# A gated cross-attention and top-2 expert kernel: first masks in six pieces, q transposed later, normalising ahead of scatters, tails cleared after 14 batches

## The reference, cut to what matters

```python
# x: 16 batches x 100 queries x 128; ctx: 16 x 1444 keys x 128; 8 experts, F = 512
xn  = layernorm(x)
att = xn @ w_input.T + (xn * dot_scale) @ ctx.T - 1e30 * mask[:, None, :]
x   = x + tanh(g_xattn) * softmax(att) @ ctx
xn2 = layernorm(x)
p   = softmax(xn2 @ W_router.T); gates, experts = top_k(p, 2); gates /= gates.sum()
y   = sum over e of weight_e * ((silu(xn2 @ W_gate[e].T) * (xn2 @ W_up[e].T)) @ W_down[e].T)
x   = x + tanh(g_ffn) * y
```

## Time and profile before

| what | value |
|---|---|
| time, median of 3 runs | 282.87 us (278.66, 282.87 and 322.13) |
| profiled execution: time | 280.85 us |
| profiled execution: span, first to last instruction | 278.8 us |
| PE busy | 242.4 us, 87% of the span |
| DVE, ACT, POOL busy | 144.4, 137.0, 112.2 us (52%, 49%, 40%) |
| chain that ended last | PE 70%, DMA 8%, issue 6%, DVE 5%, ACT 4%, POOL 4% |
| mean granted TensorE clock | 0.946 of full speed |
| one step of the steady attention | about 8.2 us (scores of batches 11 and 12 start at 103.52 and 111.69 us in the chain) |

### The profile page before, as it was taken

The page is one execution under the profiler, slowest core; times in us unless marked ns, Lnnn a source line. Parts: engine busy times, 40 slices in busy tenths (PEclk is TensorE's granted clock), DMA queues, the critical chain, the costliest instruction groups (busy, mean ns, idle before and its releaser), DMA issues.

```text
span 278.8 us, 5798 instructions
## 1 busy us (share of the span) xinstructions
PE 242.4 (87%) x1614; PEld 198.3 (71%) x1615; DVE 144.4 (52%) x467; ACT 137.0 (49%) x302; POOL 112.2 (40%) x197
## 2 busy tenths in 40 slices
PE   6799999999999999999978599699999999998100
PEld 6557777788777788777778387588888888887100
DVE  3434666767777767787746338223433343432024
ACT  3445455676555686655545234345545555545000
POOL 3250432157644476636374535433424223233200
PEclk9989999999999999999979979989999999999855
DMA  5875787778787888888632003221211111000164
GB/s 134 223 199 149 186 218 195 187 210 228 200 244 210 214 191 207 206 218 225 246 76 49 15 2 91 63 70 58 58 39 45 54 38 38 28 19 31 34 218 119
DMA packets 17645, 36.49 MB, mean 131 GB/s; under 512 B 3692, under 2 KB 9460, under 8 KB 17620
## 3 DMA queue, kind: packets, MB, share of 16 engines
q1 hardware_dynamic: 13580, 31.36, 43.4%
q0 software_dynamic: 2560, 3.77, 4.5%
q10 hardware_dynamic: 1480, 1.05, 1.2%
HBM read 30.89 MB, written 5.27 MB: 130 GB/s over the span
## 4 chain that ended last, share of the span: by engine, by line
PE 70%; DMA 8%; issue 6%; DVE 5%; ACT 4%; POOL 4%; SPq 0%; POOLq 0%; DVEq 0%; ACTq 0%
PE psum L1067 14%; PE psum L1046 13%; PE psum L1170 9%; PE psum L1022 7%; PE psum L1148 6%; PE psum L1150 5%; PE psum L1149 5%; PE psum L1159 4%; DMA ctx_sb<-results 3%; PE psum L1057 2%; DMA slots<-pair_rows,slot_i 2%; ACT probsT L616 2%; POOL slots L527 2%; DMA results<-y_sb,dest 2%; ACT qT L611 1%
## 5 line engine op out<-in xcount | busy, mean ns | idle before, releaser
L583 POOL DMA_INDIRECT results<-y_sb,dest x32 | 30.7, 959 | 57.1 <-DVE dest L948 25.6
L1067 PE MATMUL psum<-ctx_sb,probsT 120*100 120x128 f32 (+1 forms) x384 | 49.2, 280 | 0.0
L959 DVE SCALAR_TENSOR_TENSOR scores<-probs,row_in,psum 128x512 f32<-128x512 f32 x32 | 23.9, 747 | 42.6 <-ACT probs L691 41.3
L1067 PEld LDWEIGHTS psum<-ctx_sb,probsT 120*100 120x100 f32 (+1 forms) x384 | 44.9, 172 | 0.3 <-issue 0.2
L1046 PE MATMUL psum<-ctxT,qT 128*100 128x512 f32 (+1 forms) x96 | 43.2, 587 | 0.0
L527 POOL DMA_INDIRECT slots<-pair_rows,slot_i x32 | 33.5, 1046 | 22.6 <-DVE slot_i L846 8.4
L691 ACT ACTIVATE probs<-psum 128x512 f32<-128x512 f32 x32 | 19.1, 598 | 39.0 <-PE psum L1150 39.0
L1170 PE MATMUL psum<-w_down,hidT 128*128 x256 | 34.3, 277 | 0.8 <-ACT y_sb L706 0.6
L782 DVE CUSTOM_DVE_ANT_0 scores<-psum,maskb 100x1444 f32<-100x1444 f32 x16 | 26.6, 1660 | 13.3 <-PE psum L1046 13.3
L1170 PEld LDWEIGHTS psum<-w_down,hidT 128*128 128x128 f32 x256 | 31.5, 194 | 1.2 <-issue 1.2
L1148 PE MATMUL psum<-w_hi,rowT_hi 128*128 x64 | 29.1, 454 | 2.4 <-issue 1.0
(11 more groups left out here) (138 smaller groups left out, 372.2 us busy)
## 6 DMA issues: line engine op xcount, KB each, us to landing
ctx_sb<-in_ctx SPq DMA_DIRECT2D x16, 720.0 KB
maskb<-mask_scaled SPq DMA_DIRECT2D x14, 564.1 KB
w_raw<-in_w_experts SPq DMA_DIRECT2D x16, 256.0 KB, 6.0
row_in<-slots SPq DMA_DIRECT2D x32, 65.0 KB, 1.9
...
```

What stands on the lines that cost most here:

```text
L583: nc.gpsimd.indirect_dma_start(results, bass.IndirectOffsetOnAxis(ap=dest[:, s:s + 1], axis=0), y_sb[:, s, :], None).then_inc(y_stored[s], 16)
L1067: last = nc.tensor.matmul(attn_ps[0:Q, 0:D], probsT[0:rows[c], c, :], ctx_sb[0:rows[c], b % RING, c, :], start=(c == 0), stop=(c == CHUNKS ...
```

## The change

- First masks: the mask is padded to 1536 columns and read as 512-column pieces. ScalarE scales 38 rows x 512 in one instruction (rows 0 to 31 and, again, the six pieces at rows 32 to 37); VectorE turns rows 32 to 37 into the low halves. `select` picks high and low row together, so `add_mask` has three matmuls in place of six, and batch 0's runs ahead of `transpose_q(0)`. Scaling and storing the whole mask comes after ScalarE's evictions of context 0; context 3 is loaded behind the first `load_mask`. The tanh moves behind the first exponential, and the four warming matmuls of step 0 go.
- `transpose_q(b + 1)` moves from ahead of the transposed probabilities to behind the first group of `attend(b - 1)`, and ScalarE's copy of it to just ahead of the exponential.
- The router work of batch 13 (`transpose_xn2(13)`, `route(13)`, `top_two(13)`, `choose(6)`) leaves step 15 for the stretch behind it, as does batch 14's and 15's by about one place each; attention of batch 15 is no longer split around `transpose_rows(0, 1)`.
- GpSimd: scatter 10 moves to the head of loop step 15; normalise 14 goes ahead of scatter 12, normalise 15 ahead of scatter 13.
- Tails: 328 rows behind the counts after 14 batches, all eight by SP right after its first eight row loads, and scatter 14 (not `load_rows`) waits for them.
- `transpose_rows(8)` and its two halves move behind `transpose_hidden(6)`. The late tables are spread over tiles 3 to 6. The last four result scatters don't wait for earlier ones.

```diff
-SP_TAILS = 6
+TAIL_ROWS = 328
+TAIL_PART = 82
+    PIECES = 3
+    PIECE = mask.shape[1] // PIECES
+    LOW = 32
+    assert PIECE == 512 and K <= PIECES * PIECE and MASKED * PIECES <= LOW
+    SPREAD = TAIL_ROWS // TAIL_PART
+    assert TAIL_ROWS >= (TOKENS - PARTS[-2][1] * Q) + P - 1 and PARTS[-2][1] * Q + TAIL_ROWS <= REGION
...
-select = sb("select", [B, MASKED, Q], F32R)
-mask_hi = w_hi[0:B, 0:K]
-mask_lo = w_lo[0:B, 0:K]
+first_rows = LOW + MASKED * PIECES
+select = sb("select", [first_rows, MASKED * PIECES, Q], F32R)
+first_raw = w_lo[0:first_rows, 0:PIECE].bitcast(F32)
+first_split = w_hi[0:first_rows, 0:PIECE]
...
+    pieces = mask.rearrange("b (t n) -> (b t) n", n=PIECE)
     load_x(0)
-    sp.dma_start(mask_rows, mask).then_inc(mask_raw, 16)
+    sp.dma_start(first_raw[0:LOW, :], pieces[0:LOW, :]).then_inc(first_loaded_mask, 16)
+    sp.dma_start(first_raw[LOW:first_rows, :], pieces[0:MASKED * PIECES, :]).then_inc(first_loaded_mask, 16)
     load_ctx(0)
     load_x(1)
+    sp.dma_start(mask_rows, mask[:, 0:K]).then_inc(mask_raw, 16)
     load_ctx(1)
     load_x(2)
     load_ctx(2)
-    load_ctx(RING - 1)
     sp.wait_ge(mask_stored, 16)
     load_mask(MASKED)
+    load_ctx(RING - 1)
     load_x(3)
...
         n = i * YRING + k
         if k == EARLY:
             sp.wait_ge(late_ready, 1)
-            sp.wait_ge(tails_stored, 16 * E)
             sp.wait_ge(empty_stored, 16)
...
     def clear_tail(e):
-        at = sp.value_load(tail_row[0:1, e:e + 1], min_val=0, max_val=DUMMY)
-        sp.dma_start(slots[bass.ds(at, P), :], empty[:, :]).then_inc(tails_stored, 16)
+        at = sp.value_load(tail_row[0:1, e:e + 1], min_val=0, max_val=DUMMY - TAIL_ROWS)
+        sp.dma_start(slots[bass.ds(at, TAIL_ROWS), :].rearrange("(p r) d -> p r d", r=SPREAD),
+                     empty[0:TAIL_PART, :, :]).then_inc(tails_stored, 16)
...
-            for e in range(SP_TAILS):
+            for e in range(E):
                 clear_tail(e)
...
     for b in range(B):
+        if b == B - 1:
+            pair_landed(0)
+            scatter(b - 5)
         if b >= 2:
             root2(b - 2)
             normalise2(b - 2)
         if 5 <= b < B - 1:
             scatter(b - 5)
-        if b == B - 2:
-            pair_landed(0)
-        if B - 2 <= b:
-            scatter(b - 4)
         if b == 2 or b == 6 or b == 10:
             root1(b + 2, b + 6)
         if b + 2 < B:
             normalise1(b + 2)
-    pair_landed(1)
-    scatter(12)
+    scatter(11)
     root2(B - 2)
     normalise2(B - 2)
     pair_landed(1)
-    scatter(13)
+    scatter(12)
     root2(B - 1)
     normalise2(B - 1)
+    pair_landed(1)
+    scatter(13)
     last_gates()
+    pool.wait_ge(tails_stored, 16 * E)
     pair_landed(1)
     scatter(14)
...
-        if k % 2 == 0:
+        if k % 2 == 0 and k < LOOP_END:
             wait(pool, y_stored[(k - 1) % YRING], i * 16 + 16 * ((k + YRING - 1) // YRING) if k else 0)
...
     def step(b):
-        if 0 <= b - 1 < B:
-            if b + 1 < B:
-
-                act.wait_ge(probsT_raw, (b - 1) * GROUPS + 1)
-                copy_qT(b + 1)
+        if b >= 1:
             for g in range(GROUPS):
                 copy_probsT(b - 1, g)
-        elif b == 0:
-            copy_qT(1)
         if b + 1 < B:
             evict_ctxT(b + 1, 0)
             evict_ctxT(b + 1, 1)
-        if 0 <= b - 2 < B - 2:
+        if 0 <= b - 2 < B - 3:
             copy_xn2T(b - 2)
+        if b + 1 < B:
+            copy_qT(b + 1)
         if b < B:
             act.wait_ge(negmax_done, b + 1)
             nc.scalar.activation(probs[0:Q, :], scores[0:Q, :], ACT.Exp, bias=negmax[:, b % 2:b % 2 + 1],
                                  accum_out=rowsum[:, b % RING:b % RING + 1]).then_inc(probs_done, 1)
+            if b == 0:
+                act.wait_ge(small_loaded, 48)
+                nc.scalar.activation(tanh_g[:, :], gates_in[:, :], ACT.Tanh).then_inc(tanh_done, 1)
             if 4 <= b and b % 2 == 0:
                 exp_gap((b - 4) // 2)
...
     act.wait_ge(scale_loaded, 32)
     nc.scalar.activation(warm[:, :], wi_col[:, :], ACT.Exp)
+    act.wait_ge(first_loaded_mask, 32)
+    nc.scalar.activation(first_split, first_raw, ACT.Copy, scale=NEG).then_inc(mask_hi_done, 1)
+    copy_qT(0)
+    evict_ctxT(0, 0)
+    evict_ctxT(0, 1)
     act.wait_ge(mask_raw, 16)
     nc.scalar.activation(mask_rows, mask_rows, ACT.Copy, scale=NEG).then_inc(mask_scaled_done, 1)
     act.wait_ge(mask_scaled_done, 1)
     act.dma_start(mask_scaled, mask_rows).then_inc(mask_stored, 16)
-    copy_qT(0)
-    nc.scalar.activation(mask_hi, mask_rows, ACT.Copy).then_inc(mask_hi_done, 1)
-    evict_ctxT(0, 0)
-    evict_ctxT(0, 1)
-    act.wait_ge(small_loaded, 48)
-    nc.scalar.activation(tanh_g[:, :], gates_in[:, :], ACT.Tanh).then_inc(tanh_done, 1)
     for b in range(B):
         step(b)
...
     def tile_step(i, k):
         n = i * YRING + k
-        if 0 < k and k + 1 < T:
+        if 0 < k and k + 1 < T and k != EARLY - 1:
             rowT_high(i, k + 1)
+        if k == 2:
+            copy_xn2T(B - 1)
         if k < T:
             act.wait_ge(gate_up_raw, n + 1)
             wait(act, hidden_done, n - 1)
             nc.scalar.activation(silu[k % 2], gate_ps[k % 2], ACT.Silu).then_inc(silu_done, 1)
         if k == 0:
-            rowT_high(i, 1)
             copy_xn2T(B - 2)
         if 0 <= k - 1 < T:
             act.wait_ge(hidT_raw, n)
             wait(act, y_raw, n - 2)
             nc.scalar.activation(hidT[:, (k - 1) % 2, :], hidT_ps, ACT.Copy).then_inc(hidT_done, 1)
-        if k == 1:
-            copy_xn2T(B - 1)
+        if k == EARLY - 1:
+            rowT_high(i, k + 1)
         if k - 2 >= 0:
             s = (k - 2) % YRING
             act.wait_ge(y_raw, n - 1)
             wait(act, y_stored[s], i * 16 + 16 * ((k - 2) // YRING))
             nc.scalar.activation(y_sb[:, s, :], y_ps, ACT.Copy).then_inc(y_done, 1)

-    def between(n):
-        e = SP_TAILS + n - 4
-        if 0 <= n - 4 and e < E:
-            if e == SP_TAILS:
-                act.wait_ge(tails_ready, 1)
-            clear_tail(e)
-
-    exp_gap(LAST - 1)
     rowT_high(0, 0, first_rowT_ps)
-    nc.scalar.activation(warm[:, :], wi_col[:, :], ACT.Silu)
+    copy_xn2T(B - 3)
     for g in range(GROUPS):
         copy_probsT(B - 1, g)
-    over_tiles(act, tile_step, between)
+    exp_gap(LAST - 1)
+    nc.scalar.activation(warm[:, :], wi_col[:, :], ACT.Silu)
+    rowT_high(0, 1)
...
         b0, b1 = PARTS[p]
         at = ranks_of(p)
         dve.wait_ge(rank_raw, p + 1)
+        if p == LAST - 1:
+            nc.vector.tensor_copy(tail_row[:, :], at[:, N, :]).then_inc(tails_ready, 1)
         if p == LAST:
-            nc.vector.tensor_copy(tail_row[:, :], at[:, N, :]).then_inc(tails_ready, 1)
...
-        if b >= 2:
+        if 2 <= b < B - 1:
             top_two(b - 2)
-        if 3 <= b and b % 2 == 1:
+        if 3 <= b < B - 1 and b % 2 == 1:
             choose((b - 3) // 2)
         if b == 12:
+            tile_counts(False)
             tile_runs(False)
         if b == 14:
-            tile_tables(False)
+            tile_experts(False)
+            tile_rows(False)
         if 4 <= b and b % 2 == 0:
             gate_pair((b - 4) // 2)
         for c in split[1:]:
...
-    nc.vector.tensor_copy(select[:, :, :], identity[0:B, 0:MASKED].unsqueeze(2).to_broadcast([B, MASKED, Q])).then_inc(select_done, 1)
+    nc.vector.tensor_tensor(select[:, :, :], identity[0:first_rows, 0:MASKED * PIECES].unsqueeze(2).to_broadcast([first_rows, MASKED * PIECES, Q]),
+                            identity[0:first_rows, LOW:first_rows].unsqueeze(2).to_broadcast([first_rows, MASKED * PIECES, Q]),
+                            ALU.add).then_inc(select_done, 1)
...
-    nc.vector.tensor_tensor(mask_lo, mask_rows, mask_hi.bitcast(F32), ALU.subtract).then_inc(mask_lo_done, 1)
+    nc.vector.scalar_tensor_tensor(out=first_split[LOW:first_rows, :], in0=first_raw[LOW:first_rows, :], scalar=NEG,
+                                   in1=first_split[LOW:first_rows, :].bitcast(F32), op0=ALU.mult,
+                                   op1=ALU.subtract).then_inc(mask_lo_done, 1)
...
     def between(n):
         if n == 3:
+            tile_counts(True)
+        if n == 4:
             tile_runs(True)
-        if n == 4:
-            tile_tables(True)
+        if n == 5:
+            tile_experts(True)
+        if n == 6:
+            tile_rows(True)

...
     residual(B - 2)
+    statistics2(B - 2)
+    attention_gain(B - 1)
     rowT_low(0, 0, first_rowT_ps)
-    statistics2(B - 2)
+    top_two(B - 3)
+    choose(LAST - 1)
+    place(LAST - 1)
     gate_pair(LAST - 1)
-    place(LAST - 1)
-    attention_gain(B - 1)
+    rowT_low(0, 1)
     over_tiles(dve, tile_step, between)
...
     def transpose_q(b):
         pe.wait_ge(xn_done, b + 1)
+        wait(pe, ctxT_act, 2 * b + 1 if b else 0)
         nc.tensor.transpose(ring_ps[0][:, GROUP * Q:GROUP * Q + Q], xn[:, b % 2, :],
...
```

(61 more changed lines are left out.)

38 lines of the change are left out of this document (20 added, 18 removed).

## The result

The changed kernel takes 292.88 us (median; 290.63 to 293.63) beside 281.19 for the kernel before on the same chip: ratio 1.048, 95% interval 1.037 to 1.059. It is slower, where 262.0 us were forecast. The profiled execution has a span of 288.7 us where before's had 278.8.

A forecast was written before the change was run, and what follows sets the result against it. TensorE work was taken to bound the steady attention, GpSimd's in-order queue the late steps, with 13.3 us lost between 139 and 185 us. Gains 4.9 + 1.0 + 11.8 + 1.1 = 18.8 us: 280.85 to 262.0 us, range 257 to 271.

The forecast's parts named there:

- Tail clears: End of the attention: eight tails take 8 us to issue, landing near 158.5, before scatter 14 wants them.
- Rival D: Tail clears through SP hold scatter 14; slower than before beyond 3.7 us each, 286.5 us at 4.4 each; chance 0.04.
- First masks: Start of the kernel: earlier mask halves and three mask matmuls bring scores 0 and 1 forward; gain 4.9 us.
- rival B: Start: the clock stays low, scores 0 keep 4.21 us and another such stretch costs 1.6; 265.2 us, chance 0.12.
- The third term: Start: from the end of scores 0 to scores 1 takes about 2.9 us instead of 4.35; gain 1.4 us.
- Rival C: Early attention: the DMAs starve batch 2 or 3, losing about 2 to 3 us; 265 us, chance 0.08.
- q: Attention steps: q transposed later lets ScalarE start 0.3 us earlier per step; gain 1.0 us, between 0 and 2.0.
- End of the attention: From exponential 15 to `gate_up(8)`: reordered late work gains 12.5 us, 11.8 after a charge for slower GpSimd steps.
- less 0.4 because attention 15 now starts behind the first expert tile and `ranks(6)`: End of the attention: deduction from xn2(15)'s gain of 6.3 us, leaving minus 5.9, at about 152.5.
- rival A: Late chain: in-order queues keep half, slips and a clock fall leave 6 of 12.5 us; 268.5 us, chance 0.2.
- The charge of 0.7 us for slower GpSimd steps: End of the attention: normalise 14 and 15 slow beside VectorE, taking 0.7 us off the gain, bounds 0 and 1.5.
- End: Last result scatters: without waits scatter 31 starts near 259.35 instead of 260.42; gain 1.1 us.

The follow-up runs named there:

- 84-part run: The changed kernel with each tail as 336 rows cut in 84 parts of 4 rows instead of 328 in 82 of 4: 275.75 us, ratio 0.986.
- the one with the old start: The kernel with 112 parts, its whole new start undone to that of the kernel before, later q kept: 272.01 us, ratio 0.972.
- 112 parts: The changed kernel with each tail as 336 rows cut in 112 parts of 3 rows instead of 328 in 82 of 4: 273.36 us, ratio 0.978.
- the run with earlier tables: The kernel with 112 parts, late tile tables made behind tiles 3 to 5 instead of 3 to 6: 269.95 us, ratio 0.966.
- the runs with a mended start: Two on the kernel with 112 parts: context 0 loaded ahead of mask pieces, 271.43 us (0.971); more warming matmuls in TensorE's early pauses, 272.80 us (0.979).

## Why the prediction was wrong, point by point

- **Tail clears: the step that failed, and it decides.** "At 1 us each they are free", and "eight take 8". I took the price of a tail from the six of before, each of 128 parts, and scaled it by nothing. 82 rows on two engines cost 4 us each (147.7 to 179.9 us for eight). Rival D had the wait right: `tails_stored`, and 3.7 us a tail as the point from which the kernel is slower. At the 4.0 us measured its own sum gives some 283 us; the profiled execution took 290.63, and the rest is the other misses below. What D lacked was the reason, and so its chance was 0.04. "DMAs that are 0.08 busy" was no argument against it: idle engines do not help a transfer that is not given to them. The divisors of 82 would have said so without a run.
- **First masks, -4.9 forecast, -0.6 measured.** The parts that concern the masks hold: both halves by 6.1 us, three matmuls at 6.20. "The evictions then wait for the transposes alone" is true, but the transposes wait for context 0, whose load I had not priced. With context 0 first the forecast start of scores 0 appears (10.61). "I take it that the clock holds" failed in this execution: rival B. Its price was right at the start of the attention (3.2 us; 3.0 between two executions of the same start, scores 1 at 20.52 and 17.55), and nothing of it is left at the end, since the loads set the pace. The third term, 1.4, held (2.96 us against 2.9).
- **Rival C,** the starved batches, was right as a mechanism but named batch 2 or 3. It strikes at batch 4 or 8 where the start is quick, and the idle DMAs from 17 to 20 us are the ones that I had let context 3 wait through. But a quick start is not its only condition: a wait of 1.8 us for context 12 stands also in the 84-part run and in the one with the old start, whose scores 1 started at 20.11 and 22.02, and the latter loads context 3 early. What decides it there is open.
- **q, -1.0 forecast.** Mechanism right, size off: 2.5 us where nothing disturbs it, above my bound of 2.0, for the gap of 0.15 us is there in each step and a further 0.09 is saved at the router's matmul in every second one. In the kernel after, other waits leave 0.5 of it.
- **End of the attention, -11.8 forecast, -7.8 with 112 parts.** From scores 15 on: exponential 15 -2.2, as forecast. xn2 15 -3.2 instead of -5.9: a mis-sized term is "less 0.4 because attention 15 now starts behind the first expert tile and `ranks(6)`". Its probabilities were copied at 144.5 and it started at 146.9, and GpSimd, busy with scatter 12, took up the statistics 1.0 us late. From xn2 15 to scatter 14: 7.0, as forecast. From there to the load of tile 8: 10.6 instead of 9.4, because `late_ready` (170.1) came behind the scatters (169.1) and not "just ahead"; the run with earlier tables gives this back. From the load to `gate_up(8)`: 3.9 instead of 3.1. These are rival A's slips; 2.7 + 1.2 + 0.8 make up the difference to the 12.5 us before its charge. Part of it is this one execution: with the same code from scores 15 on, the runs with a mended start have xn2 15 at 16.9 and 16.8 us behind scores 15, where it has 18.7, and gain 9.2 and 9.6 us in this stretch. Why is open.
- **The charge of 0.7 us for slower GpSimd steps** had nothing to pay for. The power step of normalise 14 and 15 took 0.57 us before, and 0.57 us in the kernel after and with 112 parts, beside VectorE's choosing and placing; normalise 15 took 1.70 us from its first step to its last in both. The 1030 ns of the earlier trace rows was one step, at 113.7 us. So where I wrote "the trace agrees that such steps stretch", it does not.
- **End, -1.1 forecast, -0.4 measured** by the run that undoes it (its stretch of the table changed by +0.3 to -0.3). The wait is gone, but GpSimd itself needs 0.76 us from the release to the scatter, which I had put at nearly nothing.
- With the tail mended the forecast of 262.0 would still have been 11 us too low at 273.36; with tables and context 3 mended too it is 267.05, inside the range.
